# Convolution's taps multiplied into the in-projection's weights, in a Mamba layer between two halves of a feed-forward network

## The reference, cut to what matters

```python
xn = resid * rsqrt(mean(resid * resid) + eps) * norm_w
skip = einsum('bld,ed->ble', xn, skip_w)
x = einsum('bld,ed->ble', xn, in_w)                       # 512 channels e
xp = pad(x, ((0, 0), (Dc - 1, 0), (0, 0)))                # Dc = 4 taps
xc = conv_b + sum(xp[:, k:k + L, :] * conv_w[:, k] for k in range(Dc))
x = silu(xc)
delta = softplus(einsum('blr,er->ble', einsum('ble,re->blr', x, wd1), wd2) + wd2_b)
Bm = einsum('ble,ne->bln', x, wB)                         # 16 states n
Cm = einsum('ble,ne->bln', x, wC)
# for each token: h = exp(dt * A) * h + dt * xt * bt;  y = sum over n of h * ct
y = (ys + W_D * x) * silu(skip)
return resid + einsum('ble,de->bld', y, out_w)
```

## Time and profile before

| | us |
|---|---|
| median of 3 runs | 1327.8 |
| lowest, highest | 1327.64, 1327.88 |
| profiled execution, its own time | 1325.21 |
| its span, first to last instruction | 1323.4 |
| mean granted TensorE clock in it | 0.95 |
| first stage | 0 to some 188 |
| prologue of the Mamba layer | to 224.78, the first scan |
| eight segments | to some 1134 |
| last stage | to 1323.4 |

### The profile page before, as it was taken

How to read it: one execution, slowest core, us unless ns; L and a number is a source line. 1 busy time by engine, 2 the same in 40 slices (tenths; PEclk the granted TensorE clock), 3 DMA queues, 4 the chain that set the end, 5 groups by cost and what they waited for, 6 DMA issues and landing times. The chain is left out here.

```text
span 1323.4 us, 10922 instructions
## 1 busy us (share of the span) xinstructions
PE 1061.0 (80%) x2688; PEld 456.6 (35%) x2688; DVE 1184.1 (89%) x1768; ACT 774.8 (59%) x1321; POOL 872.6 (66%) x390
## 2 busy tenths in 40 slices
PE   3999746687889788888878988987897867799973
PEld 2434212233343343334334333432432422444421
DVE  3765898999999999999999999999999999576587
ACT  2656658757456566745666664665674434265665
POOL 0000004889989999998999999899999999000000
PEclk9999978799999999999989989999998889899998
DMA  6000003244543535343444444445444443000003
GB/s 207 1 1 1 1 1 113 96 160 133 170 141 130 181 112 185 127 159 128 149 169 141 165 142 149 140 126 191 139 149 162 137 177 112 0 1 1 1 1 128
DMA packets 48000, 146.56 MB, mean 111 GB/s; under 512 B 5504, under 2 KB 14336, under 8 KB 47936
## 3 DMA queue, kind: packets, MB, share of 16 engines
q1 hardware_dynamic: 47440, 145.03, 33.1%
q10 hardware_dynamic: 496, 0.82, 0.2%
HBM read 141.05 MB, written 4.72 MB: 110 GB/s over the span
## 5 line engine op out<-in xcount | busy, mean ns | idle before, releaser
L1155 POOL TENSOR_TENSOR late<-m_dx,m_brow 128x1024 f32<-128x1024 f32 x256 | 597.7, 2363 | 6.7 <-DVE m_a_bank L1285 6.5
L957 ACT ACTIVATE m_a_bank<-m_delta,m_negA 128x512 f32<-128x512 f32 x512 | 335.1, 683 | 174.6 <-DVE m_hc L1297 134.0
L1442 PE MATMUL m_y_bank<-m_hc,ident 128*128 128x512 f32 x640 | 332.4, 645 | 116.1 <-DVE m_hc L1297 115.4
L1167 POOL TENSOR_TENSOR m_hc_pool<-m_hid,m_crow 128x1024 f32<-128x1024 f32 x96 | 226.8, 2363 | 31.0 <-DVE m_hid L1285 30.6
L1442 PEld LDWEIGHTS m_y_bank<-m_hc,ident 128*128 128x128 f32 x640 | 119.6, 201 | 305.1 <-DVE m_hc L1297 186.7
L1297 DVE TENSOR_TENSOR m_hc<-m_a_bank,m_crow 128x512 f32<-128x512 f32 x320 | 203.0, 677 | 0.0
L1285 DVE TENSOR_TENSOR_SCAN m_a_bank<-m_a_bank,m_carry,late 128x512 f32<-128x512 f32 x160 | 196.4, 1274 | 1.1 <-ACT m_a_bank L957 0.8
L1285 DVE TENSOR_TENSOR_SCAN m_a_bank<-m_a_bank,late 128x512 f32<-128x512 f32 x160 | 186.7, 1212 | 7.0 <-ACT m_a_bank L957 3.7
L1442 PE MATMUL m_y_bank<-m_hc_pool,ident 128*128 128x512 f32 x384 | 188.0, 613 | 4.9 <-POOL m_hc_pool L1167 4.9
L1176 POOL TENSOR_TENSOR m_dx<-m_delta,m_x 128x1024 f32<-128x1024 f32 x16 | 38.0, 2377 | 216.5 <-ACT m_delta L1047 216.5
L1285 DVE TENSOR_TENSOR_SCAN m_hid<-m_a_bank,m_carry,late 128x512 f32<-128x512 f32 x96 | 117.7, 1269 | 0.0
(11 more groups left out here) (148 smaller groups left out, 1237.9 us busy)
## 6 DMA issues: line engine op xcount, KB each, us to landing
m_brow<-bc_rows SPq DMA_DIRECT2D x128, 512.0 KB, 5.0
m_crow<-bc_rows SPq DMA_DIRECT2D x128, 512.0 KB, 4.1
x_tok<-x_in SPq DMA_DIRECT2D x4, 1024.0 KB, 8.6
out<-x_tok SPq DMA_DIRECT2D x3, 1024.0 KB, 4.8
w<-w_in SPq DMA_DIRECT2D x1, 1024.0 KB, 11.6
out<-x_tok SPq DMA_DIRECT2D x4, 256.0 KB, 2.1
w<-w_in SPq DMA_DIRECT2D x1, 750.0 KB, 10.4
w<-w_in ACTq DMA_DIRECT2D x1, 512.0 KB, 6.0
```

The source lines that it names most:

```text
L957: nc.scalar.activation(a_bank[K % 2][:, j, :], delta[:, i % 2, c, :], ACT.Exp, scale=negA[:, c, n:n + 1]).then_inc(S["a"], 1)
L1155: nc.gpsimd.tensor_tensor(u[:, K % U_RING, :, :], dx[:, i % 2, 2 * q:2 * q + 2, :], brow[:, K // 2 % ROW_RING, K % 2, :].unsqueeze(1).to_b ...
L1167: nc.gpsimd.tensor_tensor(hc_pool[:, before % POOL_RING, :, :], hid[:, before % POOL_RING, :, :], crow[:, K // 2 % ROW_RING, K % 2, :].uns ...
L1442: op = nc.tensor.matmul(y_bank[:, j, :], ident[:, :], source[:, before % ring, j, :], start=False, stop=K % PASS == PASS - 1)
```

## The change

The taps are multiplied into the weights of the in-projection once, so that a chunk of the convolution is a sum of eight products: for each of four taps, weights times tap, with tokens shifted by 0 to 3 columns, for each of two blocks of 128 features. All is accumulated in PSUM. Both halves of a batch entry lie side by side in `xn`, so that the second half's shifted products read the last columns of the first. `convolve`, `keep_spill` and the table `conv` go; `accumulate` only adds the bias.

The weights `taps` are made in the first stage: SyncE loads the in-projection's weights as a tensor of their own, then one row of taps that is spread over all partitions into a buffer of the first stage (`a1[:, 1]`), and GpSimd multiplies them, eight products of 128x512. VectorE waits for these before it first writes that buffer, at the second batch's first update.

`POOL_N` goes from six states of 16 to five, so VectorE weighs eleven instead of ten. `accumulate` moves to units 2, 4, 5 and 7. Four small products on VectorE (`norms`, 128x16) are written as SCALAR_TENSOR_TENSOR.

```diff
-    POOL_N = (0, 2, 5, 7, 10, 12)
+    POOL_N = (0, 3, 6, 9, 12)
...
-        "in": ((0, 0), (1, 1), (3, 3), (4, 4)),
+        "in": ((0, 0, 1, 1), (1, 2, 2, 3), (3, 3, 4, 4), (4, 5, 5, 6)),
...
-    EARLY_TURN = ((4,), (5,))
+    EARLY_TURN = ((7,), (8,))
+
+    TAP_ORDER = [(0, 0)] + [(back, d) for back in range(1, TAPS) for d in range(KD)] + [(0, 1)]
...
-        "acc": (2, 3, 5, 6),
+        "acc": (2, 4, 5, 7),
...
-        "conv": (2, 3, 5, 6),
...
-        return {"turn": ("xn", 2 * p + c + 3), "out": ("out_there", 2 * (i - 1) + c + 1), "in": ("conv", KE * p + c + 1),
+        return {"turn": ("xn", 2 * p + c + 3), "out": ("out_there", 2 * (i - 1) + c + 1), "in": ("acc", KE * p + c + 1),
...
-                nc.scalar.activation(acc[:, ph, c, lo:], b[:, lo:], ACT.Identity,
-                                     scale=conv[:, c, TAPS - 1:TAPS], bias=conv[:, c, TAPS:TAPS + 1])\
-                    .then_inc(S["acc"], 1)
+                nc.scalar.activation(acc[:, ph, c, :], b, ACT.Identity, bias=col("conv_b", c)).then_inc(S["acc"], 1)
...
-                    nc.vector.tensor_tensor(square, rstd[:, ts], rstd[:, ts], ALU.mult).then_inc(S["square"], 1)
+                    nc.vector.scalar_tensor_tensor(square, rstd[:, ts], 1.0, rstd[:, ts], ALU.mult, ALU.mult)\
+                        .then_inc(S["square"], 1)
...
-                if prep(i):
-                    for c in due(k, "conv"):
-                        convolve(i, c)
...
-                elif kind in ("in", "skip"):
-                    if kind == "in" and part == 0:
+                elif kind == "in":
+
+                    if part == 0:
                         pe.wait_ge(S["xn"], 2 * p + 2)
+                    for n in (2 * part, 2 * part + 1):
+                        back, d = TAP_ORDER[n]
+                        lo, at = (back, 0) if p % 2 == 0 else (0, BANK - back)
+                        op = nc.tensor.matmul(b[:, lo:], taps[:, TAPS - 1 - back, d, c * P:(c + 1) * P],
+                                              xn[:, d, at:at + BANK - lo], start=n == 0,
+                                              stop=n == len(TAP_ORDER) - 1)
```

In the first stage and the block ahead of it:

```diff
+                    if b == 1 and tap_rows is not None:
+                        dve.wait_ge(taps_made, TAPS * KD)
...
+                rows = a1[:, 1].rearrange("p k t -> p (k t)").rearrange("p (s c) -> p s c", s=TAPS)
+                pool.wait_ge(rows_there, 16)
+                pool.wait_ge(load_sem["late_weights"], 48)
+                for s in range(TAPS):
+                    for d in range(KD):
+                        tap = mem["taps"][:, s, d, :]
+                        nc.gpsimd.tensor_tensor(tap, mem["taps"][:, TAPS - 1, d, :], rows[:, s, :], ALU.mult)\
+                            .then_inc(taps_made, 1)
...
+            if tap_rows is not None:
+                sp.dma_start(a1[:, 1].rearrange("p k t -> p (k t)"), tap_rows.to_broadcast([P, TAPS * INNER]))\
+                    .then_inc(rows_there, 16)
...
+            sp.dma_start(mem["taps"][:, TAPS - 1], ins["win"]).then_inc(load_sem["late_weights"], 16)
```

More of the change, by code:

```diff
@@ L161, in ffn @@
         first_added, first_act, added, stored = sem("first"), sem("firsta"), sem("added"), sem("stored")
+        rows_there, taps_made = sem("rows"), sem("taps")
         block = ctx.enter_context(nc.Block())
@@ L686, in setup @@
     with nc.Block() as block:
-        first = 2 * INNER
+        first = INNER
         @block.sync
@@ L1463, in build @@
             "x_tok": sb("x_tok", [P, TILES, DIM]),
+            "taps": sb("taps", [P, TAPS, KD, INNER]),
             "w256": sb("w256", [P, KD, W256_COLS]),
```

104 lines of the change are left out of this document (35 added, 69 removed).

## The result

The changed kernel takes 1435.7 us (median of 4 runs, 1434.9 to 1437.6) against 1327.7 us (1327.3 to 1327.9) of the kernel before in the same comparison: a ratio of 1.0816, 95% interval 1.0797 to 1.0835. It is slower, by 108 us; 93 were forecast. The profiled execution has a span of 1434.1 us against 1323.4, 110.7 more, and a mean granted clock of 0.95 in both.

The account below looks back on a forecast made before the run. VectorE bounds the segments' heads, GpSimd and VectorE the tails. Segments 1 to 6 +71, segment 0 +2, segment 7 0, before the first segment +18, start +2: +93 us, forecast 1420 us, range 1370 to 1465.

Parts of the forecast that it names:

- scan 5: VectorE's scan of unit 5 in a segment's head, forecast to start 23.7 us after unit 0 starts, undisturbed at 16.0.
- scan 8: VectorE's scan of unit 8 in a segment's head; chunk 3's emptying on ScalarE holds its decay to 42.6 us.
- Segments 1 to 6: Six middle segments: three even ones at +12.0 us and three odd ones at +11.6 us, together +71 us.
- The head's term: Units 0 to 9 of a segment: 51.3 us, against 39.6 in even and 42.05 in odd segments.
- the tail's: Units after 9 of a segment: +0.3 us in even tails (72.5 for 72.2), +2.4 in odd ones.
- the rival of the colder TensorE: Segment heads begin at TensorE's lower clock, +3.4 us in each of seven, +24: 1445 us, chance 0.12.
- The prologue: Before the first segment: nothing hides TensorE's 32 products, first scan at 243.0 us instead of 224.78, +18 us.
- The start: Before and in the first stage: more loads on SyncE, +2 us (between 1 and 6); GpSimd's building of taps 0.
- Segment 0: First segment: TensorE gets a lead of 7.0 us, head 45.9 us against 44.3; with the tail +2 us.
- The lighter wait: Segments: ScalarE's emptyings cost nothing, only rings of weighed states hold VectorE; -50 us, 1370 us, chance 0.08.
- the totals: Segments: only TensorE's whole work counts, 107.5 us a segment or 112 at lower clock; 1339 us, chance 0.05.
- The other side: Segments: TensorE's slack takes the products and VectorE's gain stays, -29 us, 1299 us, chance 0.05.

Follow-up runs that it names:

- The kernel with one chunk: Kernel before, with one of four channel chunks convolved on TensorE, the others on VectorE: 1326.9 us with the last chunk, 1325.6 us with the first.

## Why the prediction was right, and where it was not

**Direction and mechanism: right.** TensorE's list of units 0 to 6 was the bound, and ScalarE's emptyings in front of the decays carried it to VectorE. The head of segment 2 was forecast at 51.3 us and took 51.96; scan 5 at 23.7 and came at 24.6; scan 8 at 42.6 and came at 43.45; VectorE's stalls were forecast at 8, 3.5 and 6 us and are 7.99, 3.34 and 6.27. The dose of TensorE's work shows the cause, not only the trace: 16 of the 24 added products taken away, 13.0 us of a segment gone. That the delay passes through the place of the emptyings in ScalarE's list is read from the traces; no run moved the emptyings alone. There was no luck in the total: nearly all misses lie on the same side.

**Segments 1 to 6, +71 forecast, +78.6 measured.** The head's term was right within 0.7 us but in segment 3, the tail's was mis-sized. The prediction let TensorE catch up and gave the even tail 72.5 us; it took 73.4. VectorE's work there is even less than forecast (71.90 us), but it waits once more, 1.5 us, in unit 21 for a decay on ScalarE:

```profile
592.92 1.23 DVE L1297 TENSOR_TENSOR_SCAN m_a_bank<-m_a_bank,late 128x512 f32<-128x512 f32 x1 [1.52 <-ACT m_a_bank L976]
```

This wait belongs to the split of the states and not to TensorE. With half of the taps and five states on GpSimd it is 1.52 us too; with all taps on TensorE and six states on GpSimd it is 0.36, and before the change it was 0.35. ScalarE's softplus with two table loads stands ahead of this decay (587.36 to 592.13), and behind a decay that waits until VectorE is done with unit 18; the change gave VectorE the weighing of just that unit.

Even segments came out 13.5 to 13.6 us longer (12.0 forecast), odd ones 11.7 to 14.1 (11.6 forecast). Of the 14.1, in segment 3, some 2 us are the rival of the colder TensorE, in one segment out of six: its first product of a tap starts 4.3 us behind VectorE's unit 0 there and 2.0 in segment 5. Windows ahead of segment 3 and, at the same place, of segment 5:

```profile
622.00:626.00 4.00, 3.05 (x6) 0.91 (x5) 4.00 (x6) 2.02 (x5) 4.00 (x3) 0.61 0.53 144
626.00:630.00 4.00, 4.00 (x7) 1.68 (x6) 4.00 (x6) 2.06 (x5) 4.00 (x3) 0.54 0.43 171
```

```profile
876.00:880.00 4.00, 2.56 (x7) 1.01 (x6) 4.00 (x6) 2.02 (x5) 4.00 (x3) 1.00 0.55 159
```

TensorE had gone through the same short rests in both; in one the clock fell to about the lower level (1.2 GHz) and its queue entered the head 2.3 us later, in the other it didn't. What decides that, I can't tell.

**The prologue, +18 forecast, +17.7 measured.** Its in-projection, 9.36 us in the earlier trace rows, takes 29.11, and dx starts 28.85 us later, of which 9.2 come from the first stage:

```profile
206.90 29.11 PE L1381 MATMUL m_a_bank<-m_xn,taps 128*128 128x512 f32 x64 [2.29 <-ACT m_xn L1020]
...
246.84 2.36 POOL L1186 TENSOR_TENSOR m_dx<-m_delta,m_x 128x1024 f32<-128x1024 f32 x1 [207.28 <-ACT m_delta L1057]
```

**The start, +2 forecast, +9.2 measured: the step that failed.** The prediction said that what VectorE normalises between 30 and 42 us "for TensorE's transposes has some 10 us to spare". That was true and not enough. It priced GpSimd's products by whom they block, VectorE, and asked only for the next reader of what VectorE normalises. It didn't ask for what VectorE does next in its own list: the statistics of batches 2 and 3, whose square root stands in ScalarE's list ahead of TensorE's next operand. The bound was named (10.1 us without the cover), but the cover was looked for on one path only. Of the 9.2 us, 4.3 are the slower normalising and 1.4 the lower clock behind TensorE's wait, which the prediction had as a rival for the segments but not here; TensorE's first transposes and first product add some 0.6. GpSimd's part, taken away, gave 4.9 in the medians. VectorE's later start was +3.0, inside the named 1 to 6.

The rule of the Trainium skill on the port pair that the prediction weighed (SBUF — State Buffer, § SBUF: two separate sides) agrees with these rows: a normalising that takes 0.33 us by itself takes 1.28 to 1.34 from its start to the next one's while GpSimd's 1.26 us products run, one for each product (the first, begun in the middle of a product, takes 0.74), and 0.32 again behind the last of them. It agrees too on the small products written in the other form, which saved nothing:

```profile
274.81 4.58 DVE L1226 SCALAR_TENSOR_TENSOR m_roots<-m_rstd 128x16 f32<-128x16 f32 x1
```

**Segment 0, +2 forecast, +4.8 measured.** The head took 47.1 us where 45.9 were forecast, and the wait at unit 21 (1.51 us) is here too.

**Rivals.** The lighter wait and the totals fell: no wait of VectorE for TensorE's addings stands among the long ones. The other side fell at the point named for it, a product's two records of 0.43 us each. The kernel with one chunk shows what the other side looks like when its condition is met: the extra work fits into the slack of the head, and VectorE keeps its gain.

**The last stage, 0 forecast, +1.2 measured.** Nothing in it was changed. Windows of the changed kernel and, at the same place ahead of the end, of the kernel with half of the taps:

```profile
1408.00:1412.00 4.00, 3.99 (x7) 1.53 (x8) 4.00 (x13) 1.88 (x4) 0.00 (x0) 0.58 0.79 262
...
1307.10:1311.10 4.00, 3.03 (x8) 0.98 (x8) 3.97 (x11) 2.79 (x6) 0.00 (x0) 1.00 0.70 232
```

The granted clock fell here in this execution, after the same rests of 0.8 to 1.3 us in TensorE's work as in the other. It did so in five of the twelve profiled executions of this document, in no order that follows the kernels; in them the last stage takes 191.6 to 191.9 us, in the other seven 189.9 to 190.5. With segment 3 and the first stage, lower clocks make some 5 of the 18 us by which the profiled execution missed the sum.

## What to carry to other kernels

Before work is moved to an engine with a low share of busy time, take the stretch in which the work has to be done and count what that engine has free there: here 6.4 us of a head of 39.6, for 20.6 us of work, while the page showed it idle a fifth of the time. A move of 5.2 us was free in the segments and, once the prologue was spared, gave 0.5%. The next 5.2 us made a segment 4.1 to 4.6 us longer, and 10.3 more another 6.8 to 7.6, through a third engine that keeps other engines' operands behind its wait. When a neighbour slows an engine down, follow that engine's own list past the slowed instruction, not only the reader of its result.

## What the runs showed of the hardware

- Eight products of 128x512 in float32 took GpSimd 10.12 us and VectorE 5.03 us. Run on GpSimd "beside" VectorE they cost VectorE 4.3 us in eight normalisings of 128x256, nearly what VectorE needs to make them itself: one normalising went through for each of GpSimd's products.
- TensorE's granted clock was 0.61 and 0.54 of full in two windows of 4 us ahead of one segment and stayed at 1.00 ahead of another with the same pattern of rests; such a fall came in the prologue of another run (0.55), in the last stage of five executions out of twelve (1 to 2 us each), and in the first stage after a rest of 4.70 us (1.4 us).
- The first stage's weights, three loads issued on ScalarE's queue by 2.5 us, landed at 9.04 us before and at 10.11 in the changed kernel (8.7 to 9.0 us in the five kernels that keep the in-projection's weights with the others, 9.7 to 10.4 in the seven that load them as a tensor of their own). SyncE waits for them ahead of the second load of tokens, so this moved the start of everything by 1.1 us in the changed kernel. Why they land later I haven't found.
